# Experts' stage of a routed feed-forward kernel: the first bias ahead of the next rows' low part, weight copies behind y, register loads moved

## What is computed

```
logits = einsum(layernorm(x), router_w) + router_b
top_w, top_idx = top_k(logits, 2); top_w = softmax(top_w)
for e in range(8):
    h = layernorm(x, ln_g[e], ln_b[e])
    h = gelu(einsum('bld,di->bli', h, w1[e]) + b1[e])     # 256 -> 1024, exact gelu
    h = einsum('bli,id->bld', h, w2[e]) + b2[e]           # 1024 -> 256
    out = out + combine[..., e:e + 1] * h
x = layernorm(x + out)
```

## Time and profile before

| | |
|---|---|
| median of three runs | 3150.65 us |
| the profiled execution | 3151.65 us, its span 3149.9 us |
| TensorE, VectorE, ScalarE, GpSimd busy | 95%, 90%, 82%, 22% of the span |
| experts' stage | about 2672 to 3143 us of the span, 71 tiles |

### The profile page before, as it was taken

The page is one execution under the profiler, slowest core; times in us unless marked ns, Lnnn a source line. Parts: engine busy times, 40 slices in busy tenths (PEclk is TensorE's granted clock), DMA queues, the critical chain, the costliest instruction groups (busy, mean ns, idle before and its releaser), DMA issues. The chain is left out here.

```text
span 3149.9 us, 77321 instructions
## 1 busy us (share of the span) xinstructions
PE 2979.6 (95%) x30985; PEld 1273.6 (40%) x30986; DVE 2845.6 (90%) x3044; ACT 2597.6 (82%) x4831; POOL 688.8 (22%) x732
## 2 busy tenths in 40 slices
PE   8999999999999999999999999999999995999994
PEld 4433333333333333333333333333333274888884
DVE  3589999999999999999999999999999678777775
ACT  3259999999999999999999999999999944655564
POOL 2000101111011101010111111011101155667675
PEclk9989999999999999999999999999999996999997
DMA  6530202020211202020202021020201165222224
GB/s 160 125 58 29 49 22 42 29 49 28 59 29 42 42 29 42 32 42 22 42 16 35 26 47 30 27 35 22 35 25 49 41 248 202 42 44 43 42 42 130
DMA packets 104921, 169.64 MB, mean 54 GB/s; under 512 B 22232, under 2 KB 65104, under 8 KB 101936
## 3 DMA queue, kind: packets, MB, share of 16 engines
q1 hardware_dynamic: 88720, 146.81, 18.3%
q0 software_dynamic: 15904, 18.66, 3.7%
HBM read 96.74 MB, written 68.68 MB: 53 GB/s over the span
## 5 line engine op out<-in xcount | busy, mean ns | idle before, releaser
L1047 DVE TENSOR_REDUCE half_max<-scores 128x2 f32<-128x1024 f32 x2016 | 2296.6, 1216 | 10.8 <-PE scores L801 4.9
L972 ACT ACTIVATE probs<-bank 128x512 f32<-128x512 f32 x4012 | 2141.8, 595 | 143.3 <-PE bank L814 45.8
L873 PE MATMUL bank<-probs,V 128*32 128x256 f32 x16384 | 1309.6, 391 | 44.2 <-ACT probs L972 42.4
L801 PE MATMUL scores<-K,Q 48*128 48x512 f16 x4032 | 793.9, 388 | 3.0 <-SPq L554 2.2
L814 PE MATMUL bank<-Q,K 50*128 50x512 f16 x4012 | 790.0, 380 | 0.0
L873 PEld LDWEIGHTS bank<-probs,V 128*32 128x32 f32 x16384 | 322.5, 108 | 582.5 <-issue 517.0
L801 PEld LDWEIGHTS scores<-K,Q 48*128 48x128 f16 x4032 | 194.2, 93 | 834.4 <-DVE half_max L1047 532.0
L814 PEld LDWEIGHTS bank<-Q,K 50*128 50x128 f16 x4012 | 371.4, 94 | 183.9 <-ACT probs L972 4.3
L685 POOL TENSOR_SCALAR max_parts<-row_max 128x16 f16<-128x16 f32 x64 | 16.2, 253 | 1963.3 <-DVE row_max L1053 1963.3
L1617 PE MATMUL pre<-xp,w 128*128 128x128 f16 x3408 | 202.0, 219 | 19.8 <-DVE xp L1712 12.6
L1617 PEld LDWEIGHTS pre<-xp,w 128*128 128x128 f16 x3408 | 191.8, 98 | 32.7 <-issue 32.5
(11 more groups left out here) (203 smaller groups left out, 1520.4 us busy)
## 6 DMA issues: line engine op xcount, KB each, us to landing
join_rows<-in_L_ffn_w_dram SPq DMA_DIRECT2D x32, 512.0 KB, 6.7
attended<-att SPq DMA_DIRECT2D x64, 256.0 KB, 2.4
Q<-q_parts SPq DMA_DIRECT2D x96, 128.0 KB, 6.3
K<-k_parts SPq DMA_DIRECT2D x96, 128.0 KB, 6.8
values<-attended SPq DMA_DIRECT2D x6, 2048.0 KB, 9.1
q_parts<-parts SPq DMA_DIRECT2D x64, 128.0 KB, 2.4
k_parts<-parts SPq DMA_DIRECT2D x64, 128.0 KB, 2.4
w_parts<-join_rows SPq DMA_DIRECT2D x16, 512.0 KB, 7.9
```

The lines of the kernel that those rows point to most:

```text
L801: mm = nc.tensor.matmul(scores[:, b, h, :], Q[p][r, c, up, t * P:(t + 1) * P], K[p][r, up, kc * TC:(kc + 1) * TC], start=True, stop=True)
L873: mm = nc.tensor.matmul(banks[att_bank[s // KB]][32 * u:32 * u + 32, q], V[wp][:, wk, u // 2, :], probs[:, 4 * s % RING + u, q], start=(wk ...
L972: nc.scalar.activation(probs[:, i % RING, :], banks[tile_bank[i]][:], ACT.Exp, scale=SCALE).then_inc(exp_done, 1)
L1047: nc.vector.tensor_reduce(half_max[lc % 2][:, :, up, t, kc], scores[:, b], AX.X, ALU.max).then_inc(max_done[b], 1)
```

## The change

On VectorE a step is written in another order: weights for tile n+3, then the register load for the bias, low part of h for n+1, bias for n+2, low part of x for n+3, y for n. Across steps, the weight copy for a tile thus stands just behind y where it stood just ahead of it, and the bias stands ahead of the low part of x. On ScalarE the operations stand in the same order as before, but the step begins one operation earlier: the register load for `norm_rows` is made before `weigh` of the previous tile in place of after it. The diff, with the opening tiles:

```diff
@@ scalar
-            def norm_rows(n, p):
-                e = owner(act, n)
+            def norm_rows(n, p, e):
                 act.wait_ge(turned, n + 1)
...
             def step(n, it, q, left):
                 p = q % 2
                 if left >= 3:
-                    norm_rows(n + 3, 1 - p)
+                    e = owner(act, n + 3)
+                if later(n, 1):
+                    weigh(n - 1, it + (q - 1) // GB, (q - 1) % GB)
+                if left >= 3:
+                    norm_rows(n + 3, 1 - p, e)
                 if left >= 2:
                     gelu(n + 2, p)
-                weigh(n, it, q)
...
             run(act, step)
+            weigh(USED - 1, (USED - 1) // GB, (USED - 1) % GB)
@@ vector
-            def add_b1(n, p):
-                e = owner(dve, n)
+            def add_b1(n, p, e):
...
             def step(n, it, q, left):
                 p = q % 2
+                if left >= 3:
+                    take_w1(n + 3, 1 - p)
+                if left >= 2:
+                    e = owner(dve, n + 2)
                 if left >= 1:
                     h_low(n + 1, 1 - p)
+                if left >= 2:
+                    add_b1(n + 2, p, e)
                 if left >= 3:
                     x_low(n + 3, 1 - p)
-                if left >= 2:
-                    add_b1(n + 2, p)
-                if left >= 4:
-                    take_w1(n + 4, p)
                 e = owner(dve, n)
...
             x_low(1, 1)
-            add_b1(0, 0)
             take_w1(2, 0)
+            add_b1(0, 0, owner(dve, 0))
             x_low(2, 0)
-            add_b1(1, 1)
-            take_w1(3, 1)
+            add_b1(1, 1, owner(dve, 1))
             h_low(0, 0)
```

More of the change, by code:

```diff
@@ L1680, in step @@
                 if left >= 3:
-                    norm_rows(n + 3, 1 - p)
+                    e = owner(act, n + 3)
[3 more added lines that the diff above has]
+                    norm_rows(n + 3, 1 - p, e)
                 if left >= 2:
                     gelu(n + 2, p)
-                weigh(n, it, q)
-            norm_rows(0, 0)
-            norm_rows(1, 1)
-            norm_rows(2, 0)
+            for n in range(3):
+                norm_rows(n, n % 2, owner(act, n))
             gelu(0, 0)
```

## The result

The changed kernel takes 3115.5 us (median of four runs, 3114.7 to 3117.12) against 3150.31 for the kernel before (median of four): ratio 0.9889, 95% interval 0.9872 to 0.9906, a gain of 1.1%. The profiled execution took 3117.12 us (span 3115.2), 34.5 less than that of before. The forecast was 3120, range 3114 to 3140, so the time lies in the range, close to its lower end.

What follows compares the result with a forecast made beforehand. A closed ScalarE-VectorE chain was taken to bound at 6.03 us per tile; TensorE's 5.52 plus 0.03 and 0.03 gives 5.58, 65 periods gain 29.5, the opening 1.7, together 31.2 us: 3120, range 3114 to 3140.

Steps and rivals of the forecast that it cites:

- a closed chain through ScalarE and VectorE: Experts' stage: waits from bias add to next bias add, through gelus, ys, xgT, xp and x_low, set the 6.02 us period.
- The bias ahead of x_low: VectorE's step: takes x_low, xgT, xp and ys out of the chain, leaving 4.5 us; called the main avoidable share.
- The copy behind y: VectorE's weight copy: w1 buffer filled about 1 us later at no cost, y and ys earlier; no gain counted.
- VectorE's sum of 5.4: VectorE's own work per tile, two exposed loads and the branch: 5.4 us, bounds 5.2 and 5.65, under TensorE's 5.52.
- ScalarE's idle before h: Sign that the forecast is right: ScalarE's wait for the bias add, 2.21 us before, falls below 2 us.
- The misses of 0.03 and 0.03: Added to TensorE's 5.52 us per tile: 0.03 for lateness in each fourth tile, 0.03 for GpSimd's queue.
- rival B: GpSimd can't get in between copy and h_low, rows come late: period 6.3, slower at 3167 us; chance 0.12.
- the 1.0 us that the term left for being shut out: GpSimd's queue: 4.5 us of undisturbed work and gaps per tile leaves 1.0 of the period; GpSimd held stable.
- Rival A: VectorE or GpSimd become the bound above 5.66 us per tile: period 5.73, 3130 us (3126 to 3141); chance 0.22.
- C: Nothing comes of it: the chain closes otherwise, period stays at 6.0, 3150 us; chance 0.06.
- The opening: Stage's start: py(0) 2.4 us earlier, 1.0 lost waiting for x_low(3), 1.7 gained at the turn of tile 5.
- The tail: End of the experts' stage, a chain of scatters: unchanged, gain 0.

Runs made afterwards that it cites:

- e6: The kernel before with 16 matmuls into py per tile instead of 24 (third term of the second product left out): 3151.54 us, ratio 1.0006.
- e3: The kernel before with only ScalarE's register load moved ahead of ys: 3130.38 us, ratio 0.9939.
- e5: The kernel before with only the weight copy moved behind y, and h_low(0) ahead of the copy for tile 3: 3129.24 us, ratio 0.9935.
- e12: The kernel before with the edits of e3 and e5 together: 3127.13 us, ratio 0.9926.
- e2: The kernel before, order of operations kept, with VectorE's bias load moved ahead of x_low and ScalarE's load ahead of ys: 3117.5 us, ratio 0.9898.
- e1: The kernel before with the bias add moved ahead of x_low, its register load thereby placed behind h_low: 3120.81 us, ratio 0.9909.
- e4: The kernel before with only VectorE's register load for the bias moved behind h_low: median 3123.31 us, ratio 0.9913; four runs from 3118.73 to 3128.3.
- e7: The changed kernel with the third term of the second product left out (16 matmuls into py, not 24): 3118.15 us, ratio 0.9904.
- e11: The changed kernel run once more, unaltered, on the chip of e10: 3115.75 us, ratio 0.9888.
- e8: The kernel of e2 with the third term of the second product left out (16 matmuls into py, not 24): 3096.7 us, ratio 0.9831.
- e9: Against e7, still with 16 matmuls into py: weight copy between x_low and y, apart from h_low; bias ahead of x_low: 3103.27 us, ratio 0.9844.
- e10: The kernel of e2 with h_low(0) ahead of the copy for tile 3 and the gelu table loaded before the first rows: 3115.43 us, ratio 0.9884.

## Why the prediction was right, point by point

**What bounds.** Right: a closed chain through ScalarE and VectorE, TensorE's floor 5.52 (5.53 measured over 65), no change of clock; e6 shows that TensorE had no share. The chain itself was incomplete. Its link from ys to xgT was read as a load of 0.25; it was the end of a second way over the copy and y, 0.35 us longer than the way over the gelus is without it (e3, e5, e12).

**The bias ahead of x_low** was called the most important share. That isn't borne out. It is not necessary (e2), and in the one run that has it alone (e1) it comes with a load moved out of the chain, which by itself did as well in two of e4's four runs. The 65 periods of the changed kernel (359.46 us) are no shorter than those of e2 (358.83), which has the loads alone. So no run shows that the swap as such is worth anything. The parts of the change overlap, and each alone brings 19 to 29 us of the 35. This was the weakest sentence of the prediction: the terms of its own sum, 0.40 and 0.25 of loads against the 0.50 that separate 6.02 from 5.52, could have told. That the time came out all the same is in part luck: the change also moves the loads, and TensorE's floor ends the gain whichever part brings it.

**The copy behind y** was costed at nothing. Alone it is worth 19 us (e5); in the full change it adds nothing that could be told.

**VectorE's sum of 5.4.** The load behind y idles 0.67 in the tile shown, not 0.41, and 0.34 early in the stage; from y to copy it is 1.17 on average. The sum, 1.17 + 1.14 + 1.14 + 1.14 + 0.83, is 5.42. y waits for TensorE, as it said. ScalarE's idle before h, which was to fall below 2 us, is 1.97 on average and up to 2.2, hardly less than before: that sign told nothing.

**The misses of 0.03 and 0.03** were oversized. The period is 5.51 or 5.52 in three tiles of four and about 5.55 in the fourth: 0.01 together. That term is 65 x 0.05 = 3.3 us. The forecast of 3120 lay 3 us over the profiled execution and 4.5 over the median. The forecast gain of 31.2 is 3.5 short of the 34.7 in span: 3.3 for this term and 1.5 for the parts put at nothing, less 1.3 for the opening.

**GpSimd** behaved as the term said, not as rival B: the gather issued during the copy (2767.67, ends 2769.67) ends 0.82 after the copy's end and inside h_low, so it got in between the two. It fills the period with no idle but keeps up: the 1.0 us that the term left for being shut out is what that gather takes up, 2.00 in place of 0.99. Rival A's mechanism is real, but one size further down: it sets in once TensorE needs less (e7). C is refuted by the result.

**The opening** was mis-sized: 1.7 forecast, 0.43 measured. py(0) is 1.13 us earlier (12.85 against 13.98 after the first turn), not 2.4: only the copy between u(1) and h_low(0) has left its way. u(1) starts 10.35 after the first turn in both kernels, because it waits for the second gelu of tile 0 (there is one u), which the working overlooked. Nor does the copy now ahead of u(0) cost anything: the first gelu starts 8.2 after the first turn in both, behind ScalarE's table load of 1.28. Of the 1.13, 0.70 is lost again between the turns of tiles 4 and 5, where the wait for x_low(3) was foreseen at 1.0 (0.53 idle before pre(3)). The tail, put at 0, gave 0.83 (56.89 to 56.06, and 56.17 in e11), of which the cause wasn't looked for. The 0.66 ahead of the stage is within what two runs of one kernel differ by.

## What to carry to other kernels

When engines wait for each other in a ring, write down every way around it, those over registers and buffers too; with several of like length, edits that look additive aren't, and the gain ends where the next engine's own time begins. A register load runs from the moment at which the instruction ahead of it in the queue is handed over (0.25 us after y's end behind ys, 0.11 after y's start in most tiles for the one behind y), not from when the engine idles: put it behind an operation that is long and whose semaphore comes early. Before keeping an order because it is fast, lighten the engine that bounds: two orders of equal time here (ratios 0.9889 and 0.9898) differ by 21 us behind it (e7 and e8, one chip).

## What the runs showed of the hardware

- An indirect gather on GpSimd takes 0.99 us undisturbed. Issued while VectorE's float16 copy of 128 x 4096 or its two-input h_low runs, it ends 0.80 to 0.88 us after that one ends, in nearly all cases of the six timelines counted (before, changed, e4, e7, e9, e10); it can slip in between two that are back to back. A scatter whose later part meets the copy ends some 0.1 us after it in most tiles and takes up to 2.7 us (e7) in place of 1.62.
- Register loads are longer beside the later part of GpSimd's rows gather. In the changed kernel VectorE's load lasts 0.30 to 0.32 us beside a scatter, a gather of shares or nothing, and up to 0.67 beside a rows gather; the held ones end some 0.2 us before the gather does. So the copy behind y starts 0.21 to 0.26 us after the gather's end in three tiles of four (2767.62 after 2767.36, above), and in e4 xgT 0.30 to 0.35 after it. In e7, where the rows gather lies elsewhere, the same copy starts 0.43 to 0.45 after y's end in two tiles of four, in place of 0.7, and 0.90 after it at the branch in both. No run took the gather away by itself, so this is what the timelines show side by side and not a tested cause.
